# Shared experts' units spread past the mixer loop, the carried part of y scaled on ScalarE, x's normalised rows one chunk an iteration

## The chip, the cores and the metric

One core of one Trainium2 chip runs the whole program. The metric is device microseconds of one execution; the time before is the median of three runs. In the text PE is TensorE, PEld its weight loads, DVE VectorE, ACT ScalarE, POOL GpSimd, SP SyncE.

## The reference, cut to what matters

8 sequences of 1,024 tokens, model width 128. A Mamba-2 mixer (4 heads of 64, state 128), a residual with layer norm, a mixture of experts (14 routed with top 2, and 2 shared, hidden width 256), and a residual with layer norm again:

```python
zxbcdt = x @ in_proj_w                      # z 256, xBC 512, dt 4
xBC = silu(conv4(xBC) + conv_b)
# per token: state = state * exp(A dt) + (x dt) B ;  y = C . state
g = (y + D x) * silu(z);  g = g * rsqrt(mean(g**2) + eps) * norm_w
x = layernorm(x + g @ out_proj_w)
shared = sum over 2 experts of  silu(rmsnorm(x) * rw @ W1) @ W2
routed = gated sum over the top 2 of 14 experts of the same
x = layernorm(x + shared + routed)
```

## The kernel before

The 8,192 tokens are 64 chunks of 128 (`NC`), eight chunks a sequence (`CPB`), four chunks a tile (`NT` = 16 tiles). Every engine has its own program, written out by hand, and all run the same loop: iteration `i` from -5 to 83 (`LAST` = 84), in which each step works on a chunk or tile that lies a fixed number of iterations back. The order in which steps stand in the loop is the order of each engine's queue, and semaphores tie the engines together.

**The mixer, iterations up to 66.** In iteration i PE projects z of chunk i-1 (line 761), turns x and B of chunk i token-major (768), projects one of four 128-channel blocks of a tile (776), turns the gated g of chunk i-4 (782), does one unit of the shared experts, the out projection of chunk i-5 (809), and then the scan in its chunk form: gram (844), addition to the state (847), and y of chunk i-2 (857, 860), to which the carried part, the state times C, is written in the other half of the same PSUM bank (864; not in a sequence's first chunk). ACT empties z (946) and x and B (955, four instructions of 64 columns, each scaled by a per-partition dt; 958), applies the convolution's first tap and silu (971, 975, 963), sums g squared (980), copies gT (983), applies silu to the unit's hidden values (992). Every fourth iteration (i mod 4 = 3) it also writes the four normalised chunks of a tile into `rows` (1001, 1003) and normalises x itself in place, four instructions (909); one iteration later (i mod 4 = 0) it copies xnT (1009). DVE does three convolution taps (1117), the running decay (1125), the mix (1130), the state (1143), and for chunk i-3 y: the carried part times `into` (1151), plus the inside part (1154), times silu(z) (1160). `in_turn` takes one instruction of each of these chains in rotation.

**Units of the shared experts.** Unit u (`shared_units`) does on PE the first product of hidden block u (802, two matmul records) and, from u = 4 on, the second product of one chunk of the tile before (793, eight records). There are 68 units, one an iteration in iterations 16 to 83.

**PSUM banks.** `act_ring` and `dve_ring` give three banks each in the order in which uses are listed (`act_uses`, `dve_uses`). A use waits until the use three places before it has been released. So PE's gT (782) waits for ACT's zs of the same iteration (946), and PE's hidden product (802) for ACT's bt of the same iteration (958).

**The routed part.** Slots of 128 rows are read back from DRAM sorted by expert (`slots_in`), four tiles a group, 36 groups (`gr`). Groups 0 to 10 have their steps in iterations 69, 71, 73, 75 and 77 to 83, the rest stand behind the loop. A group costs PE four transposes (717), 8 hidden matmuls (728, 16 records) and 8 down matmuls (748, 16 records), ACT two silus (920), DVE two PSUM copies and four weight picks (1396, 1408, 1419), and POOL four indirect DMAs (602) that return the rows to DRAM. During the last iterations POOL also issues the indirect DMAs that dispatch rows (661). `xT`'s memory is used again by the routed part, once the hidden products that read it are done (`AREA_UNITS`).

Of the kernel before, what the change touches and what calls it, by code (L numbers as in the profile page):

```python
# [11 lines left out]
ALU = mybir.AluOpType  # L12
ACT = mybir.ActivationFunctionType
AX = mybir.AxisListType
P = 128
# [17 lines left out]
    "mix", "y_carried", "y_sum", "skip_diag", "gated", "residual", "ln_stats", "shift",  # L33
# [3 lines left out]
    "rate", "dt_exp", "chunk_decays", "step_decay", "rows_copied", "xbc_raw", "xbc_silu", "z_silu", "xdt", "g_squares", "bt",  # L37
# [34 lines left out]
def mamba_moe(nc, xT_d, x_d, w_in_d, conv_w_d, conv_b_d, norm_w_d, w_out_d, dt_bias_d, a_log_d,  # L72
# [75 lines left out]

    def shared_units(i):
        return [i - LAG] if 0 <= i - LAG < NC + 4 else []  # L150
# [66 lines left out]
    for gr in range(GROUPS_IN_LOOP, GROUPS):  # L217
        if gr + 2 < GROUPS:
            dve_uses.append(("slotsT", gr + 2))
        if gr + 1 < GROUPS:  # L220
            act_uses += [("routed", n2) for n2 in pairs_of(gr + 1)]
        dve_uses.append(("down", gr))

    with ExitStack() as ctx:
# [107 lines left out]
        carve, used = carver(xT[:])  # L332
        slots_out = [carve(W) for _ in range(3)]
# [339 lines left out]
        def tensor_program(e):  # L673
# [78 lines left out]

            dt_raws(*STEPS[0])
            for i in range(FIRST, LAST):
# [29 lines left out]
                for u in shared_units(i):  # L784
                    if u >= 4:
                        t, c4 = divmod(u - 4, 4)
                        on.wait_ge("hidden_silu", 4 * t + 4)
                        on.wait_ge("w2_loaded", 16)
                        on.wait_ge("shared_added", t)
                        on.wait_ge("dt_raw_added", 3)  # L790
                        for n in range(NSH):
                            e_no, k = divmod(n, HB)
                            mm = e.matmul(down_bank[:, c4 * P:(c4 + 1) * P], hid[(4 * t + n) % NHID][:, c4 * P:(c4 + 1) * P], w2_shared[:, e_no, k, :],  # L793
                                          start=(n == 0), stop=(n == NSH - 1))
                        mm.then_inc(S["down"])
                    if u < NC:
                        t, n = divmod(u, 4)
                        e_no, k = divmod(n, HB)
                        on.wait_ge("w1_scaled", NE - NR)
                        on.wait_ge("xnT_copied", t + 1)  # L800
                        bank = act_bank("hidden", u)
                        e.matmul(bank[:], w1_shared[:, e_no, k * P:(k + 1) * P], xnT[t], start=True, stop=True).then_inc(S["hidden"])  # L802
# [73 lines left out]
            for gr in range(GROUPS_IN_LOOP, GROUPS):  # L876
                routed_group(gr)
# [3 lines left out]
        def scalar_program(e):  # L881
# [53 lines left out]

            dt_exp(0)
            for i in range(FIRST, LAST):
# [46 lines left out]
                for u in shared_units(i):  # L984
                    if u < NC:
                        on.wait_ge("hidden", u + 1)

                        was = u - NHID
                        if was >= 0:
                            on.wait_ge("down", 4 * (was // 4) + 4)  # L990
                        on.wait_ge("dt_step", 3 * DT_CHAIN)
# [647 lines left out]
```

## Time and profile before

| | before |
|---|---|
| median of 3 runs (lowest, highest) | 784.41 us (782.98, 786.55) |
| the profiled execution's own time | 785.97 us |
| its span in the profile | 784.2 us |
| granted PE clock over the span | 0.924 |
| PE / PEld busy | 658.8 us (84%) / 557.2 us (71%) |
| DVE / ACT / POOL busy | 608.7 (78%) / 444.4 (57%) / 497.6 us (63%) |

Read it by stage: the mixer loop lies between about 60 and 470 us, the routed part behind it. A busy share over the whole span mixes the two. The profiled execution is 1.6 us above the median.

### The profile page before, as it was taken

To read this page: it belongs to the slowest core of one execution; us is meant where nothing else is said; L and a number is where in the kernel's file an instruction comes from. 1 tells how busy PE (TensorE), PEld (TensorE's weight loads), DVE (VectorE), ACT (ScalarE), POOL (GpSimd) and SP (SyncE) were. 2 spreads that over 40 slices of the span, in tenths; PEclk is the share of its full clock that TensorE was granted. 3 is DMA by queue.
4 is the path that set the end of the run, shared out by engine and by line. 5 is a ranking of instruction groups with operands and counts; after the bars stand their busy time and mean duration, and the time that the engine had idled before them with its cause. 6 is when DMAs were issued, how large, how long until landed. Compare 5 with 4: busy or idle time off the path is not lost.

```text
span 784.2 us, 14802 instructions
## 1 busy us (share of the span) xinstructions
PE 658.8 (84%) x4299; PEld 557.2 (71%) x4299; DVE 608.7 (78%) x1838; ACT 444.4 (57%) x1225; POOL 497.6 (63%) x545
## 2 busy tenths in 40 slices
PE   5987888999999999999999998886697877776840
PEld 4865676787787787787778887675587877665730
DVE  4899889999999999999999887337236342588875
ACT  4875777868767867877876754411113111335645
POOL 1144454887787787777887875566565656555652
PEclk9899999999999999999999999897799989898875
DMA  8541111121111221111221127123323222555436
GB/s 299 190 135 41 43 39 31 64 59 55 61 51 58 65 58 55 52 62 59 58 62 48 35 85 247 48 61 90 82 72 85 82 83 80 163 146 158 139 95 214
DMA packets 62639, 70.76 MB, mean 90 GB/s; under 512 B 10335, under 2 KB 45285, under 8 KB 62304
## 3 DMA queue, kind: packets, MB, share of 16 engines
q1 hardware_dynamic: 52656, 52.79, 23.2%
q0 software_dynamic: 8608, 16.87, 6.3%
q8 instruction: 36, 0.59, 0.3%
q14 instruction: 43, 0.35, 0.2%
q10 hardware_dynamic: 1296, 0.16, 0.1%
HBM read 48.55 MB, written 23.01 MB: 91 GB/s over the span
## 4 chain that ended last, share of the span: by engine, by line
PE 44%; issue 13%; ACT 11%; DVE 11%; another core or an unknown queue 4%; DMA 2%; SPq 2%; POOL 0%; DVEq 0%; ACTq 0%; POOLq 0%
PE bank L793 6%; PE bank L728 5%; PE bank L748 5%; PE bank L802 4%; PE bank L860 4%; ACT x L909 3%; PE bank L776 2%; PE bank L847 2%; ACT rows L1001 2%; PE bank L857 2%; PE bank L809 2%; PE bank L761 2%; PE bank L864 2%; DVE xbcT_area L1117 2%
## 5 line engine op out<-in xcount | busy, mean ns | idle before, releaser
L602 POOL DMA_INDIRECT returned<-xT,slots_in x141 | 142.7, 1012 | 102.5 <-DVE xT L1419 62.2
L661 POOL DMA_INDIRECT dispatched<-rows,row_u x128 | 147.2, 1150 | 31.6 <-issue 31.3
L1117 DVE SCALAR_TENSOR_TENSOR xbcT_area<-raw,conv_w,xbcT_area 128x512 f32<-128x512 f32 x162 | 125.5, 776 | 2.5 <-ACT xbcT_area L975 2.4
L728 PE MATMUL bank<-xT 128*128 128x128 f32 x564 | 85.0, 308 | 30.3 <-issue 12.8
L920 ACT ACTIVATE raw<-bank 128x512 f32<-128x512 f32 (+1 forms) x71 | 39.9, 588 | 117.2 <-remote 78.9
L728 PEld LDWEIGHTS bank<-xT 128*128 128x128 f32 x564 | 79.0, 221 | 34.6 <-issue 19.7
L1419 DVE COPY xT<-bank 128x512 f32<-128x512 f32 (+1 forms) x36 | 24.4, 678 | 101.1 <-remote 87.6
L748 PE MATMUL bank<-xbcT_area,raw 128*128 x564 | 83.3, 301 | 16.8 <-issue 16.0
L748 PEld LDWEIGHTS bank<-xbcT_area,raw 128*128 128x128 f32 x564 | 76.9, 214 | 20.6 <-issue 20.6
L1125 DVE TENSOR_TENSOR_SCAN decay_area<-decay_area,ident_heads 128x512 f32<-128x512 f32 x64 | 87.3, 1365 | 0.0
L946 ACT ACTIVATE zs<-bank 128x256 f32<-128x256 f32 x64 | 24.3, 379 | 110.0 <-PE bank L761 110.0
L793 PE MATMUL bank<-w_shared,hid 128*128 128x128 f32 x512 | 73.9, 284 | 13.5 <-issue 13.5
L793 PEld LDWEIGHTS bank<-w_shared,hid 128*128 128x128 f32 x512 | 66.6, 199 | 17.0 <-issue 16.8
L909 ACT ACTIVATE x<-x,shift,rstd 128x128 f32<-128x128 f32 x128 | 52.1, 480 | 39.4 <-issue 34.4
L649 POOL TENSOR_TENSOR state_kept<-state,whole 128x256 f32<-128x256 f32 x56 | 46.6, 833 | 41.2 <-DVE state L1143 25.5
L860 PE MATMUL bank<-xdt,mix 128*128 128x128 f32 x512 | 69.9, 281 | 0.0
L802 PE MATMUL bank<-xT,w_shared 128*128 128x512 f32 x128 | 68.3, 616 | 0.7 <-ACT bt L958 0.2
L776 PE MATMUL bank<-xT,w_in 128*128 128x512 f32 x128 | 66.9, 609 | 0.0
L593 POOL TENSOR_TENSOR xend<-xdt,outof 128x256 f32<-128x256 f32 x64 | 65.9, 1030 | 1.3 <-ACT xdt L955 1.2
L860 PEld LDWEIGHTS bank<-xdt,mix 128*128 128x128 f32 x512 | 64.6, 198 | 0.0
L955 ACT ACTIVATE xdt<-bank,dt 128x64 f32<-128x64 f32 x256 | 59.2, 313 | 1.6 <-PE bank L768 1.6
L992 ACT ACTIVATE hid<-bank 128x512 f32<-128x512 f32 x64 | 40.3, 629 | 33.0 <-remote 15.9
(232 smaller groups left out, 1531.0 us busy)
## 6 DMA issues: line engine op xcount, KB each, us to landing
decay_area<-decay_rows SPq DMA_DIRECT2D x64, 256.0 KB
slots_in<-dispatched SPq DMA_DIRECT2D x141, 64.5 KB
hid<-returned SPq DMA_DIRECT2D x18, 256.0 KB
xT<-xT_dram SPq DMA_DIRECT2D x8, 512.0 KB, 8.1
x<-x_dram SPq DMA_DIRECT2D x8, 512.0 KB, 7.9
out_dram<-x SPq DMA_DIRECT2D x16, 256.0 KB
xT<-returned SPq DMA_DIRECT2D x14, 256.0 KB
returned<-xT,slots_in POOLq DMA_INDIRECT x141
```

The source lines that it names most:

```text
L593: e.tensor_tensor(xend[h][:].rearrange("p (n s e) -> p n s e", s=2, e=HD), xdt[c % len(xdt)][:].rearrange("p n (s e) -> p n s e", e=HD)[:, ...
L602: e.indirect_dma_start(returned, bass.IndirectOffsetOnAxis(ap=slots_in[sb_][:, n, D:ROW].bitcast(U32), axis=0), slots_out[b][:, n * P:(n + ...
L661: e.indirect_dma_start(dispatched, bass.IndirectOffsetOnAxis(ap=row_u[t % 2][:, m:m + 1], axis=0), rows[t % 3][:, k, c4, :], None).then_in ...
L728: mm = e.matmul(bank[:, off:off + P], w1_now[b][:, k * P:(k + 1) * P], slotsT[gr % len(slotsT)][:, n % 4 * P:(n % 4 + 1) * P], start=True, ...
L748: mm = e.matmul(bank[:, j * P:(j + 1) * P], hidden_r[n2 % len(hidden_r)][:, off:off + P], w2_routed[:, bass.ds(experts[4 * (gr % 2) + j], ...
L776: e.matmul(bank[:], w_in[:, DI + k * P:DI + (k + 1) * P], xT[:, t * W:(t + 1) * W], start=True, stop=True).then_inc(S["xbc"])
L793: mm = e.matmul(down_bank[:, c4 * P:(c4 + 1) * P], hid[(4 * t + n) % NHID][:, c4 * P:(c4 + 1) * P], w2_shared[:, e_no, k, :], start=(n == ...
L802: e.matmul(bank[:], w1_shared[:, e_no, k * P:(k + 1) * P], xnT[t], start=True, stop=True).then_inc(S["hidden"])
L860: mm = e.matmul(bank[:, n * P:(n + 1) * P], mix[h][:, k, :], xdt[c % len(xdt)][:, n, zero_first * HD:zero_first * HD + P], start=False, st ...
L909: e.activation(x[:, 4 * t + c, :], x[:, 4 * t + c, :], ACT.Identity, scale=rstd[:, t, 0, c:c + 1], bias=shift[:, t, 0, c:c + 1]).then_inc( ...
L1117: e.scalar_tensor_tensor(o, r[:, n:n + W], conv_w[:, k, TAPS - 1 - n:TAPS - n], o, ALU.mult, ALU.add).then_inc(S["conv"])
L1125: e.tensor_tensor_scan(flat(running[c % 2]), flat(decay_all[b]), flat(ident_heads[:]), 0.0, ALU.mult, ALU.add).then_inc(S["running"])
```

## The change

Three edits, with nothing changed in what is computed.

1. `shared_units` follows a table: one unit an iteration, but none where i mod 4 = 3 up to iteration 64; two in iterations 68, 70, 72, 74 and 76; the last seven stand beside groups 11 to 17 behind the loop. At the end of iteration 64, 37 units are done where 49 were, and 61 at the end of iteration 83, where there were 68. The memory carved out of `xT` is ordered anew, with one wait for each piece.
2. The carried part times `into` moves from DVE (one instruction of 256 columns) to ACT (four instructions of 64 columns, one a head, per-partition scale), behind zs and ahead of xdt. DVE's addition now waits for ACT.
3. x is normalised one chunk an iteration, in iterations 12 to 75, instead of four chunks in each fourth iteration.

```diff
+    units = {i: 1 for i in range(LAG, LAST + NC) if i > NC or i % 4 != 3}
+    for i in range(NC + 3, min(ROUTED_AT[-1], NC + 13)):
+        if i not in ROUTED_AT:
+            units[i] = 2
+    unit_ends, units_so_far = {}, 0
+    for i in sorted(units):
+        units_so_far = min(units_so_far + units[i], NC + 4)
+        unit_ends[i] = units_so_far
+
     def shared_units(i):
-        return [i - LAG] if 0 <= i - LAG < NC + 4 else []
+        return range(unit_ends.get(i - 1, unit_ends.get(i - 2, 0)), unit_ends[i]) if i in unit_ends else []
+
+    def beside_group(gr):
+        return LAST + gr - GROUPS_IN_LOOP
...
@@ the memory carved out of xT
+        w1_now = [carve(HB * P) for _ in range(8)]
+        slotsT = [carve(W) for _ in range(3)]
+        SLOTST_UNITS = units_of(0)
+        OUT_UNITS = [units_of((b + 1) * W) for b in range(3)]
         slots_out = [carve(W) for _ in range(3)]
-        slotsT = [carve(W) for _ in range(3)]
-        w1_now = [carve(HB * P) for _ in range(8)]
         gexp = carve(NC * NR).rearrange("p (c r) -> p c r", c=NC)
-        AREA_UNITS = 4 * -(-used[0] // W)
+        GEXP_UNITS = units_of(0)
...
@@ TensorE (ScalarE and VectorE likewise)
             for gr in range(GROUPS_IN_LOOP, GROUPS):
+                shared_experts(beside_group(gr))
                 routed_group(gr)
...
@@ ScalarE
-            def normalise(t, signal):
-                for c in range(4):
+            def normalise(t, signal, chunks=range(4)):
+                for c in chunks:
...
+                c = i - 3
+                if at(i, 3, NC) and c % CPB:
+                    on.wait_ge("y_out", c + 1)
+                    on.wait_ge("chunk_decays", 3 * steps_range(c) + 3)
+                    on.wait_ge("y_sum", kept_upto(c) - 1)
+                    for k in range(NH):
+                        e.activation(y_carried[:, k * HD:(k + 1) * HD], dve_ring.bank("out", c)[:, DI + k * HD:DI + (k + 1) * HD], ACT.Copy,
+                                     scale=into[:, c, k:k + 1]).then_inc(S["y_carried"])
...
-                    normalise(t, "x1")
+                t, c = divmod(i - 12, 4)
+                if 0 <= t < NT:
+                    normalise(t, "x1", (c,))
...
@@ VectorE
                 if c % CPB:
-                    on.wait_ge("chunk_decays", 3 * steps_range(c) + 3)
-                    e.tensor_tensor(heads(y_carried[:]), heads(bank[:, DI:2 * DI]), per_head(into[:, c, :]), ALU.mult).then_inc(S["y_carried"])
-                    yield
-                    on.wait_ge("y_carried", kept_upto(c))
+                    on.wait_ge("y_carried", NH * kept_upto(c))
                     e.tensor_tensor(y_inside[:], bank[:, 0:DI], y_carried[:], ALU.add).then_inc(S["y_sum"])
```

ACT's queue in one iteration with i mod 4 = 3 and the start of the next, in the middle of the mixer, before:

```order
L946 ACTIVATE zs<-bank 128x256
L955 ACTIVATE xdt<-bank,dt 128x64 x4
L958 ACTIVATE bt<-bank 128x128
...
L983 ACTIVATE gT<-bank 128x256
L992 ACTIVATE hid<-bank 128x512
L1001 ACTIVATE rows<-x,shift,rstd 128x128 x4
L1003 ACTIVATE rows<-rows 128x4x128
L909 ACTIVATE x<-x,shift,rstd 128x128 x4
L946 ACTIVATE zs<-bank 128x256
```

The same stretch of the changed program:

```order
L982 ACTIVATE zs<-bank 128x256
L990 ACTIVATE y_carried<-bank,into 128x64 x4
L1000 ACTIVATE xdt<-bank,dt 128x64 x4
L1003 ACTIVATE bt<-bank 128x128
...
L1028 ACTIVATE gT<-bank 128x256
L1038 ACTIVATE rows<-x,shift,rstd 128x128 x4
L1040 ACTIVATE rows<-rows 128x4x128
L934 ACTIVATE x<-x,shift,rstd 128x128
L982 ACTIVATE zs<-bank 128x256
```

hid has left this iteration, three of the four x have gone to the other iterations, and four y_carried stand between zs and xdt in every iteration but one in eight.

PE's queue behind the loop, where group 11 follows group 10, before (the last down matmul of one group, then the next group):

```order
L748 MATMUL bank<-xbcT_area,raw 128x128
L717 MATMUL bank<-ident,slots_in 128x128 x4
L728 MATMUL bank<-xT 128x128 x8
L416 TENSOR_LOAD expert_late
```

and in the changed program a unit stands ahead of the group's transposes:

```order
L769 MATMUL bank<-xbcT_area,raw 128x128
L784 MATMUL bank<-w_shared,hid 128x128 x4
L793 MATMUL bank<-xT,w_shared 128x512
L738 MATMUL bank<-ident,slots_in 128x128 x4
L749 MATMUL bank<-xT 128x128 x8
L437 TENSOR_LOAD expert_late
```

Where a matmul has float32 operands, the trace shows two records for each of these rows' instructions.

## Rows read from the trace of the kernel before

**Rows 1.** Busy time by engine, four mixer iterations (start:end length, then engines)

```profile
293.00:321.00 28.00, 27.40 (x186) 22.18 (x183) 27.07 (x73) 21.07 (x63) 21.91 (x24) 1.00 0.18 55
```

**Rows 2.** Chain that ended last, 232 to 243 us (start, length, what)

```profile
232.65 0.43 PE bank L761 x2
...
236.89 0.49 ACT hid L992
...
239.85 1.17 ACT x L909 x3
241.02 0.36 ACT zs L946
...
242.81 0.86 PE bank L802 x2
```

**Rows 3.** Timeline of ACT, an iteration's start, and bt of an early one

```profile
311.39 0.38 ACT L946 ACTIVATE zs<-bank 128x256 f32<-128x256 f32 x1 [3.10 <-PE bank L761]
311.72 0.93 ACT L955 ACTIVATE xdt<-bank,dt 128x64 f32<-128x64 f32 x4
312.53 0.29 ACT L958 ACTIVATE bt<-bank 128x128 f32<-128x128 f32 x1
...
130.38 0.29 ACT L958 ACTIVATE bt<-bank 128x128 f32<-128x128 f32 x1
```

**Rows 4.** Timeline of PE: z and hidden product of these two iterations

```profile
310.76 0.59 PE L761 MATMUL bank<-w_in,xT 128*128 128x256 f32 x2
...
313.49 1.02 PE L802 MATMUL bank<-xT,w_shared 128*128 128x512 f32 x2
...
130.81 1.10 PE L802 MATMUL bank<-xT,w_shared 128*128 128x512 f32 x2 [0.20 <-ACT bt L958]
```

**Rows 5.** Group of DVE's carried part (count, busy us, mean ns, idle before)

```profile
L1151 DVE TENSOR_TENSOR y_carried<-bank,into 128x256 f32<-128x256 f32 x56 | 22.3, 399 | 3.2 <-PE bank L864 3.1
```

**Rows 6.** Timeline of DVE in that iteration, state and carried part

```profile
309.19 0.42 DVE L1143 TENSOR_TENSOR state<-bank,state_kept 128x256 f32<-128x256 f32 x1 [0.64 <-PE bank L847]
...
311.33 0.40 DVE L1151 TENSOR_TENSOR y_carried<-bank,into 128x256 f32<-128x256 f32 x1
```

**Rows 7.** Timeline of POOL, first and last of two bursts of eight DMAs

```profile
643.60 1.07 POOL L602 DMA_INDIRECT returned<-xT,slots_in  x1 [2.99 <-DVE xT L1419]
652.73 0.97 POOL L602 DMA_INDIRECT returned<-xT,slots_in  x1 [0.30 <-issue]
656.67 1.07 POOL L602 DMA_INDIRECT returned<-xT,slots_in  x1 [2.96 <-DVE xT L1419]
```

**Rows 8.** Timeline of PE over the first of these bursts

```profile
643.93 1.06 PE L717 MATMUL bank<-ident,slots_in 128*128 128x128 f32 x4
644.79 3.21 PE L728 MATMUL bank<-xT 128*128 128x128 f32 x16
647.84 1.95 PE L748 MATMUL bank<-xbcT_area,raw 128*128 x16
649.62 0.60 PE L717 MATMUL bank<-ident,slots_in 128*128 128x128 f32 x4
650.06 1.95 PE L728 MATMUL bank<-xT 128*128 128x128 f32 x16
652.98 0.27 PE L748 MATMUL bank<-xbcT_area,raw 128*128 x1 [0.44 <-issue]
655.13 1.48 PE L748 MATMUL bank<-xbcT_area,raw 128*128 x11 [0.44 <-issue]
```

**Rows 9.** Timeline of DVE: the copy that ends this wait

```profile
655.20 0.69 DVE L1419 COPY xT<-bank 128x512 f32<-128x512 f32 x1 [8.54 <-remote]
```

**Rows 10.** Chain that ended last, one unit in iteration 70

```profile
493.27 0.89 PE bank L793 x8
494.17 0.86 PE bank L802 x2
```

**Rows 11.** Timeline of PE: its wait behind the tables of iteration 76

```profile
547.73 3.75 PE L728 MATMUL bank<-xT 128*128 128x128 f32 x16 [4.80 <-DVE xT L1396]
```

More of the change, by code:

```diff
@@ L217, in mamba_moe @@
     for gr in range(GROUPS_IN_LOOP, GROUPS):
+        act_uses += [("hidden", u) for u in shared_units(beside_group(gr)) if u < NC]
         if gr + 2 < GROUPS:
@@ L751, in routed_group, with shared_experts @@
                 mm.then_inc(S["routed_down"])
+            def shared_experts(i):
+                for u in shared_units(i):
+                    if u >= 4:
+                        t, c4 = divmod(u - 4, 4)
+                        on.wait_ge("hidden_silu", 4 * t + 4)
+                        on.wait_ge("w2_loaded", 16)
+                        on.wait_ge("shared_added", t)
+                        on.wait_ge("dt_raw_added", 3)
+                        for n in range(NSH):
+                            e_no, k = divmod(n, HB)
+                            mm = e.matmul(down_bank[:, c4 * P:(c4 + 1) * P], hid[(4 * t + n) % NHID][:, c4 * P:(c4 + 1) * P], w2_shared[:, e_no, k, :],
+                                          start=(n == 0), stop=(n == NSH - 1))
+                        mm.then_inc(S["down"])
+                    if u < NC:
+                        t, n = divmod(u, 4)
+                        e_no, k = divmod(n, HB)
+                        on.wait_ge("w1_scaled", NE - NR)
+                        on.wait_ge("xnT_copied", t + 1)
+                        bank = act_bank("hidden", u)
+                        e.matmul(bank[:], w1_shared[:, e_no, k * P:(k + 1) * P], xnT[t], start=True, stop=True).then_inc(S["hidden"])
             dt_raws(*STEPS[0])
@@ L783, in tensor_program @@
                     tr.then_inc(S["gT"])
[L784 to L802, printed above, removed]
+                shared_experts(i)
                 c = i - 5
@@ L934, in by_token, with hidden_of_shared @@
                     normalise(s - 2, "x2")
+            def hidden_of_shared(i):
+                for u in shared_units(i):
+                    if u < NC:
+                        on.wait_ge("hidden", u + 1)
+                        was = u - NHID
+                        if was >= 0:
+                            on.wait_ge("down", 4 * (was // 4) + 4)
+                        on.wait_ge("dt_step", 3 * DT_CHAIN)
+                        e.activation(hid[u % NHID][:], act_ring.bank("hidden", u)[:], ACT.Silu).then_inc(S["hidden_silu"])
             dt_exp(0)
@@ L983, in scalar_program @@
                     e.activation(gT[c % 2][:].rearrange("p k i -> p (k i)"), act_ring.bank("gT", c)[:, 0:DI], ACT.Copy).then_inc(S["gT_copied"])
[L984 to L991, printed above, removed]
-                        e.activation(hid[u % NHID][:], act_ring.bank("hidden", u)[:], ACT.Silu).then_inc(S["hidden_silu"])
+                hidden_of_shared(i)
                 t = due(i, 11)
@@ L1417, in routed_group @@
                     on.wait_ge(f"returned{b}", 64 * (gr // len(slots_out)))
+                on.wait_ge("hidden", OUT_UNITS[b])
                 cols = slice(0, len(slot_tiles(gr)) * P)
@@ L1423, in gates_before @@
                 best = top_v[:, :, 0:1]
+                on.wait_ge("hidden", GEXP_UNITS)
                 e.tensor_tensor(rms_of[:], rstd[:, :, 0, :], rstd[:, :, 1, :], ALU.mult).then_inc(S["gate"])
@@ L1509, in by_token, with shared_add @@
                             ln_shift(u, 1, 3 * NT + 2 * n + 2)
+            def shared_add(i):
+                for u in shared_units(i):
+                    if u >= 4 and u % 4 == 3:
+                        t = (u - 4) // 4
+                        on.wait_ge("down", 4 * t + 4)
+                        on.wait_ge("x1", 4 * t + 4)
+                        e.tensor_tensor(x[:, 4 * t:4 * t + 4, :], down_bank[:].rearrange("p (c d) -> p c d", c=4), x[:, 4 * t:4 * t + 4, :], ALU.add).then_inc(S["shared_added"])
             later = steps_of(0)
@@ L1559, in vector_program @@
                     ln_shift(t, 2, 3 * t + 3)
-                for u in shared_units(i):
-                    if u >= 4 and u % 4 == 3:
-                        t = (u - 4) // 4
-                        on.wait_ge("down", 4 * t + 4)
-                        on.wait_ge("x1", 4 * t + 4)
-                        e.tensor_tensor(x[:, 4 * t:4 * t + 4, :], down_bank[:].rearrange("p (c d) -> p c d", c=4), x[:, 4 * t:4 * t + 4, :], ALU.add).then_inc(S["shared_added"])
+                shared_add(i)
                 if i == NC + 2:
@@ L1572, in vector_program @@
                 if n == 1:
-                    on.wait_ge("hidden", AREA_UNITS)
+                    on.wait_ge("hidden", SLOTST_UNITS)
                     for gr in range(2):
@@ L1583, in vector_program @@
                     gates_before()
+                shared_add(beside_group(gr))
                 routed_group(gr)
```

7 lines of the change are left out of this document (5 added, 2 removed).

## The prediction

> **What bounds the kernel now.** I read the busy time by stage first, then the chain that ended last, then the timelines around the waits in that chain. The reader should see that no engine has room to spare in the mixer on average, but that the chain changes engine in one iteration of four.
>
> In four mixer iterations PE is busy for 27.40 of 28.00 us and DVE for 27.07, while ACT works for 21.07 [rows 1]. So PE and DVE look like the bound. The chain says where the small rest is lost. In an iteration with i mod 4 = 3 ("the heavy iteration") it goes from PE's z at 232.65 to ACT and stays there, through hid and x at its end, until zs of the next iteration at 241.02; then PE's gT can start and at 242.81 the hidden product [rows 2]. From there it stays on PE for three iterations. One round of four iterations is thus an ACT stretch of 241.02 - 232.65 = 8.37 us and a PE stretch of the rest.
>
> Behind the loop POOL sets a rhythm: eight DMAs from 643.60 to 652.73 + 0.97 = 653.70, then a wait of 2.96 for DVE's copy, and the next burst at 656.67, a period of 13.07 us for two groups [rows 7]. PE issues 4 + 16 + 16 + 4 + 16 = 56 records in the burst, then goes on one by one, and resumes at 655.13, 1.4 us after POOL's last DMA; DVE's copy comes at 655.20, long after the down product of 647.84 was issued [rows 8, 9]. So in a burst PE can run ahead by some 56 records and then stands until POOL is through. The trace doesn't say why. The Trainium skill (TensorE: Matmul & The Clock Gate, Specifications) gives an engine queue depth of 64 for TensorE; by that rule the 56 records agree with a queue that fills up.
>
> **Edit 1, the units, in the mixer.** A round loses one unit: 8 records of the down product (0.89) and 2 of the hidden product (0.86), 1.75 us of PE [rows 10], and ACT's hid (0.49) in the heavy iteration [rows 2]. PE's part of it comes off at a place where the chain is on ACT, so only the 0.49 counts. What is late next is ACT's own queue.
>
> **Edit 3, x one chunk an iteration.** Three of four x leave the heavy iteration: 1.17 us off the ACT stretch [rows 2]. In the other three iterations ACT waits for PE's z (3.10 us in one of them [rows 3]), which hides the 0.39 that each gets; without that cover it would cost 1.17 a round and give the whole gain back.
>
> **Edit 2, the carried part on ACT.** DVE loses an instruction of 0.40, 56 times, 22.3 us [rows 5]. The new work on ACT is four instructions of 64 columns from PSUM with a per-partition scale, which is the form of xdt: four of them take 312.53 - 311.72 = 0.81 us of the queue [rows 3]. I take that. The end above it is four mean durations without overlap, 0.93 and more; the end below is nothing, if ACT waited anyway. They stand between zs and xdt, so everything behind zs comes 0.81 later: xdt, bt, silu, raw and the rest, and PE's hidden product waits for bt.
> The Trainium skill (ScalarE: Activation LUTs, What ACT_TABLE_LOAD costs) gives 186 ns, plus 93 for a pointer operand, plus 0.833 ns a column, less 93 of overlap: an estimate of 239 ns, 0.96 for four. The trace has 0.81; with 0.96 the mixer would come out 6 us dearer than below.
>
> How late is bt for PE? From zs's start to bt's end ACT needs 312.53 + 0.29 - 311.39 = 1.43 us [rows 3]; from bt's end to the hidden product, when it waits for it, 130.81 - 130.67 = 0.14 [rows 3, 4]. With the new 0.81 the hidden product can start 1.43 + 0.14 + 0.81 = 2.38 after zs.
> - Heavy iteration into the next: before, the hidden product came 242.81 - 241.02 = 1.79 behind zs [rows 2]; now 2.38, so 0.59 later.
> - The two other iterations with a unit: zs starts 0.63 behind z, the hidden product 2.73 behind z [rows 3, 4]. Now 0.63 + 2.38 = 3.01: a new wait of 0.28 in each.
>
> A round: -0.49 (hid) - 1.17 (x) + 0.81 (carried part in the heavy iteration) + 0.59 + 2 x 0.28 = +0.30. In every second round the heavy iteration's chunk is the first of a sequence and has no carried part: -0.51. The mean is -0.11, and 11 rounds (iterations 20 to 63) give -1.2 us. The 1.75 us that PE no longer works and the 0.40 of DVE turn into waits for ACT.
>
> Does DVE bound it? It gains 0.40 in three to four iterations of a round [rows 5], but its addition can't start before ACT's carried part is done, 0.63 + 0.33 + 0.81 = 1.77 behind PE's z, which here is at 312.53 [rows 3, 4]. DVE began this iteration at 309.19, ahead of z, and reached the carried part at 311.33 [rows 6], so it would wait 1.2 us there, with the mix queued behind it. Its gain pays for that; I count zero, also for the first iterations (3 to 19), where DVE is the fuller engine; bounds -5 to +4 for the whole mixer.
>
> **Edit 1, behind the mixer.** 12 units more stand after iteration 64: 12 x 1.75 = 21 us of PE at the full clock, if nothing hides them. Piece by piece:
> - Iteration 68, second unit: PE is in the chain there, as in iteration 70 [rows 10]. +1.75.
> - 70, 72, 74: each stands ahead of a group's down product, in a rhythm that POOL's bursts set. PE has about 13.07 us and needs about 8.4 for two units, a group and the small products; with a third unit 10.2. It then runs into the limit of 56 records before the down product is out, and gives 10 records after the burst. I take +1.2 for the three together (bounds 0 and 5.3).
> - 76: PE waits 4.80 us for the tables [rows 11], which hides 1.75. 0. Without that wait it would cost 1.75.
> - Groups 7 to 10 get a hidden product each (4 x 0.86 = 3.4), where PE already does a down product beside each group and a pair of groups takes about what POOL's bursts give. Half: +1.7.
> - Groups 11 to 17 get 3 whole units and 4 without a hidden product, 3 x 1.75 + 4 x 0.89 = 8.8. A pair has 72 records now, and some 82 find room in a period (56 in the burst, the rest in the 3 us between bursts at 0.11 each); a pair with units has 92 or 88. A third of the time: +2.9.
> Sum +7.6; bounds 1.75 and 21. The value is nearer the low end because POOL's 13.07 us stay as they are. The new wait values on the `xT` memory are met: 40 units are done by iteration 67, where 28 are asked for.
>
> **Sum.** -1.2 + 7.6 = +6.4 us. On the profiled execution's 785.97 us (span 784.2) that is 792.4; it lies 1.6 above the median, so the median should go from 784.4 to 790.8, say 791.
>
> **Rivals.**
> - *The mixer is freed after all.* If ACT keeps up (bt isn't late, or the heavy iteration's ACT stretch is hidden by PE's shorter queue), PE sets the round: 27.40 - 1.75 = 25.65 in place of 28.0, -2.35 a round over 12 rounds, -28 at most. It decides as soon as the ACT stretch of the heavy iteration falls under PE's. For it: ACT idles a quarter of the time [rows 1]. Against: the order in ACT's queue worked out above. With half of it and the tail's +7.6 the time is 784.4 - 14 + 7.6 = 778, in full 764.
> - *POOL's rhythm hides the units.* Only iteration 68 costs: -1.2 + 1.75 = +0.5, 785: no change. For it: the down product is issued long before the copy that waits for it [rows 8, 9].
> - *The units behind the mixer are all on the path*, as PE's record limit in a burst makes each cost more than its own time: +21, or 804.
> - *The edits don't do what they say* in the mixer, DVE's wait for ACT passes on to the mix and to PE: one wait of 1 us a round, +11, with the tail 802. The start of DVE's iteration ahead of z speaks for it, its idle time against.
>
> **How the numbers follow.** About 0.5% (3.9 us) is what a measurement of this kernel can tell from no change. Forecast (788.5 to 797): 0.42. Rhythm hides the units: 0.23. Mixer freed: 0.22. The two dear cases together: 0.13. Slower is the forecast and the dear cases less a tenth of the first's low edge, 0.52; same 0.26; faster 0.22. The range takes half of the freed mixer's cases and reaches to the dear ones: 774 to 803.
>
> **What the profile of the changed kernel would show.** Right: PE's round stays at 28 us with 25.6 busy; PE's hidden product waits for ACT's bt in most iterations; ACT's heavy iteration is followed by zs without idle time; DVE's addition waits for y_carried; the granted clock stays 1.00 in the mixer; iteration 64 ends about as early as before; POOL's bursts still come every 13 us and the last one ends 6 us later. Wrong: a round clearly under 28 us, or bursts whose period has grown by more than 1 us. The prediction fails most easily in the tail, where the third and the half are choices, and in the mixer if PE's longer waits let the clock fall.

## The result

| | before | after |
|---|---|---|
| median (lowest, highest), 4 runs each | 783.69 us (782.70, 786.55) | 811.28 us (808.27, 812.01) |
| the profiled execution / its span | 785.97 / 784.2 us | 812.01 / 810.2 us |
| zs of iteration 20 / of iteration 64 | 156.25 / 461.05 | 156.98 / 480.56 |
| a round of four iterations between them (11 rounds) | 27.71 us | 29.42 us |
| first / last DMA of the returned rows | 494.99 / 765.47 | 517.02 / 791.02 |

The changed kernel takes 1.0345 times as long (95%: 1.0313 to 1.0377), 27.6 us between the medians and 26 between the two profiled executions. By stage: +19.5 us up to iteration 64, +2.5 from there to the first returned row, +4.0 from there to the end. Nearly all of the surprise is in the mixer.

The view of busy time of the changed kernel over those 11 rounds answers to [rows 1]:

```profile
156.98:480.56 323.58, 297.11 (x1855) 243.38 (x1854) 271.60 (x757) 249.54 (x814) 233.97 (x258) 0.96 0.17 52
```

PE has 122 matmul records fewer than before (1855 against 1977) and is still busy for 297 us, at a granted clock of 0.96, and idle for 26.5. The view of waits (total us, times, longest) of the same stretch says for whom:

```profile
ACT zs L982 <- PE bank L803: 64.7, 38, 3.5
DVE y_inside L1192 <- ACT y_carried L990: 37.8, 22, 3.0
...
PE bank L868 <- DVE mix L1171: 22.8, 11, 2.9
```

DVE waits for ACT's carried part in two iterations of four, and once a round PE waits 2.1 us for DVE's mix, ahead of the gram. In the kernel before PE hardly waited for the mix (view of waits, iterations 20 to 64):

```profile
PE bank L844 <- DVE mix L1130: 0.5, 2, 0.3
```

The timelines of ACT and PE in a non-heavy iteration answer to [rows 3, 4]:

```profile
311.33 0.38 ACT L982 ACTIVATE zs<-bank 128x256 f32<-128x256 f32 x1 [1.65 <-PE bank L803]
311.61 0.92 ACT L990 ACTIVATE y_carried<-bank,into 128x64 f32<-128x64 f32 x4
312.39 0.95 ACT L1000 ACTIVATE xdt<-bank,dt 128x64 f32<-128x64 f32 x4
313.18 0.34 ACT L1003 ACTIVATE bt<-bank 128x128 f32<-128x128 f32 x1
```

```profile
310.70 0.59 PE L803 MATMUL bank<-w_in,xT 128*128 128x256 f32 x2
...
313.56 1.13 PE L793 MATMUL bank<-xT,w_shared 128*128 128x512 f32 x2
```

The four new instructions take 312.39 - 311.61 = 0.78 us (0.81 forecast), bt ends 2.19 behind zs (2.24 forecast), and the hidden product starts 2.86 behind z (3.01 forecast). ACT's queue is as I drew it. What I had not drawn comes in the next iterations, in DVE's timeline and then PE's:

```profile
320.26 0.42 DVE L1192 TENSOR_TENSOR y_inside<-bank,y_carried 128x256 f32<-128x256 f32 x1 [1.05 <-ACT y_carried L990]
...
321.38 0.68 DVE L1171 TENSOR_TENSOR mix<-decay_area,bank 128x512 f32<-128x512 f32 x1
...
325.76 1.63 DVE L1166 TENSOR_TENSOR_SCAN decay_area<-decay_area,ident_heads 128x512 f32<-128x512 f32 x1
...
328.29 0.67 DVE L1171 TENSOR_TENSOR mix<-decay_area,bank 128x512 f32<-128x512 f32 x1
```

```profile
329.11 0.46 PE L868 MATMUL bank<-xbcT_area 128*128 128x128 f32 x2 [1.98 <-DVE mix L1171]
```

DVE waits at its addition, and the mix of the same iteration stands behind it. From there DVE works almost without a gap (the router's choice is in this iteration), and its next mix ends 8.7 us after the start of the addition, when PE has been standing for 1.98. This is the heavy iteration, the one that lost its unit, so PE gets to the gram 1.75 us sooner than before. This trace alone doesn't say how much of PE's wait comes from DVE's wait and how much from the missing unit; e2 and e4 below do. And PE's wait has a price of its own. Two of the eleven waits in PE's timeline:

```profile
182.47 0.35 PE L868 MATMUL bank<-xbcT_area 128*128 128x128 f32 x1 [1.73 <-DVE mix L1171]
240.14 0.35 PE L868 MATMUL bank<-xbcT_area 128*128 128x128 f32 x1 [2.14 <-DVE mix L1171]
```

and the 4.5 us behind each of them and behind a third, in the view of busy time (the granted clock is the third number from the right):

```profile
182.47:186.97 4.50, 4.50 (x29) 3.77 (x30) 3.07 (x5) 4.47 (x16) 4.02 (x6) 1.00 0.21 75
240.14:244.64 4.50, 4.50 (x20) 4.25 (x21) 3.07 (x5) 2.99 (x9) 4.02 (x6) 0.62 0.25 70
449.05:453.55 4.50, 4.50 (x20) 4.20 (x21) 2.07 (x3) 1.16 (x3) 3.86 (x7) 0.63 0.19 61
```

The third wait was of 2.90 us. After the first the clock stays at its upper level (2.4 GHz) and 29 records fit; after the others it is 0.62 on average, most of the stretch at 1.2 GHz, and 20 fit. Seven of the eleven waits are followed by such a stretch (those of 2.14, 2.33, 2.71 and 2.90 us and three of 1.98), four are not (1.55, 1.55, 1.73 and one of 1.98): 7 x 4.5 x 0.38 = 12 us. The Trainium skill (TensorE: Matmul & The Clock Gate, HAM oscillation) describes a matmul kernel whose groups are parted by waits for DMA and start at the throttled clock each time. The trace agrees that waits which come back regularly are paid for in clock again and again; the waits in the page's example are longer than these, and that such a stretch can follow waits of 1.98 to 2.90 us is shown by this trace alone.

So the 18.8 us between iterations 20 and 64 are: PE's idle time from 5.3 to 26.5 (+21.1), the clock +12, units gone 11 x 1.75 = -19.3, and +5 that remain. The hidden product, which waits for bt, accounts for 3 of them: it is busy for 36.84 us in 33 units where it was for 45.04 in 44, that is 1.12 for 1.02 each. The other 2 I can't place.

Behind the loop POOL's timeline answers to [rows 7]: bursts of eight as before. The two shown lie 13.36 us apart; from any burst of eight to the next burst it is 13.0 to 13.5 us in both kernels, once 14.5 in the changed one.

```profile
694.86 1.07 POOL L623 DMA_INDIRECT returned<-xT,slots_in  x1 [2.89 <-DVE xT L1458]
...
703.89 0.97 POOL L623 DMA_INDIRECT returned<-xT,slots_in  x1 [0.30 <-issue]
708.22 0.97 POOL L623 DMA_INDIRECT returned<-xT,slots_in  x1 [3.36 <-issue]
```

### The profile page after: what moved, and what is told of

The parts are those of the page before. It is cut to its first block, busy times and chain, and to the rows that moved or that the text cites. A ratio compares the mean times of both kernels' runs of the same rounds, so it can differ in the third digit from the quotient of the medians.

```text
span 810.2 us, 15029 instructions
## 1 busy us (share of the span) xinstructions
PE 668.1 (82%) x4299; PEld 562.6 (69%) x4299; DVE 584.5 (72%) x1782; ACT 489.1 (60%) x1449; POOL 486.3 (60%) x545
## 4 chain that ended last, share of the span: by engine, by line
PE 43%; DVE 21%; ACT 15%; issue 14%; DMA 2%; another core or an unknown queue 2%; SPq 1%; DVEq 0%; POOL 0%; ACTq 0%; POOLq 0%
DVE xbcT_area L1158 5%; PE bank L769 5%; PE bank L749 5%; PE bank L884 5%; PE bank L784 5%; PE bank L793 5%; ACT y_carried L990 3%; PE bank L881 2%; DVE decay_area L1166 2%; PE bank L871 2%; DVE mix L1171 2%; PE bank L803 2%; PE bank L888 2%; ACT xdt L1000 2%
## 5 line engine op out<-in xcount | busy, mean ns | idle before, releaser
L682 POOL DMA_INDIRECT dispatched<-rows,row_u x128 | 143.5, 1121 | 31.7 <-issue 31.7
L1158 DVE SCALAR_TENSOR_TENSOR xbcT_area<-raw,conv_w,xbcT_area 128x512 f32<-128x512 f32 x162 | 123.3, 762 | 3.3 <-ACT xbcT_area L1020 3.3
L749 PE MATMUL bank<-xT 128*128 128x128 f32 x564 | 83.3, 306 | 26.8 <-issue 12.0
L769 PE MATMUL bank<-xbcT_area,raw 128*128 x564 | 81.5, 300 | 8.4 <-issue 7.4
L934 ACT ACTIVATE x<-x,shift,rstd 128x128 f32<-128x128 f32 x128 | 61.0, 515 | 39.4 <-DVE shift L1525 27.5
L793 PE MATMUL bank<-xT,w_shared 128*128 128x512 f32 x128 | 72.4, 647 | 7.9 <-ACT bt L1003 4.4
L884 PE MATMUL bank<-xdt,mix 128*128 128x128 f32 x512 | 73.4, 290 | 0.0
L884 PEld LDWEIGHTS bank<-xdt,mix 128*128 128x128 f32 x512 | 68.3, 207 | 0.0
L614 POOL TENSOR_TENSOR xend<-xdt,outof 128x256 f32<-128x256 f32 x64 | 61.3, 957 | 0.2 <-ACT xdt L1000 0.2
```

The costliest lines, as they stand in the source:

```text
L614: e.tensor_tensor(xend[h][:].rearrange("p (n s e) -> p n s e", s=2, e=HD), xdt[c % len(xdt)][:].rearrange("p n (s e) -> p n s e", e=HD)[:, ...
L682: e.indirect_dma_start(dispatched, bass.IndirectOffsetOnAxis(ap=row_u[t % 2][:, m:m + 1], axis=0), rows[t % 3][:, k, c4, :], None).then_in ...
L749: mm = e.matmul(bank[:, off:off + P], w1_now[b][:, k * P:(k + 1) * P], slotsT[gr % len(slotsT)][:, n % 4 * P:(n % 4 + 1) * P], start=True, ...
L769: mm = e.matmul(bank[:, j * P:(j + 1) * P], hidden_r[n2 % len(hidden_r)][:, off:off + P], w2_routed[:, bass.ds(experts[4 * (gr % 2) + j], ...
L884: mm = e.matmul(bank[:, n * P:(n + 1) * P], mix[h][:, k, :], xdt[c % len(xdt)][:, n, zero_first * HD:zero_first * HD + P], start=False, st ...
L1158: e.scalar_tensor_tensor(o, r[:, n:n + W], conv_w[:, k, TAPS - 1 - n:TAPS - n], o, ALU.mult, ALU.add).then_inc(S["conv"])
```

## The experiments

Four groups of four, each group on one chip with the kernel before beside it (medians of before: 738.95, 781.93, 782.33 and 787.22 us). "Round" is the time of four iterations, the mean of the 11 rounds between zs of iterations 20 and 64; it hardly depends on the chip (27.71 and 27.69 for the kernel before, 27.06, 27.06 and 27.02 for the third edit alone). The times expected for e1 to e4 are for a kernel before of 784 us; their chip runs it in 738.95, so the ratio is what can be compared.

| run | what | ratio to before [95%] | round, us | zs of iteration 64 |
|---|---|---|---|---|
| e5 | before again | | 27.69 | 460.74 |
| e2 | edit 1 | 1.0006 [0.9990, 1.0023] | 27.35 | 456.07 |
| e1 | edit 2 | 1.0332 [1.0292, 1.0373] | 29.35 | 483.58 |
| e3, e11, e16 | edit 3 | 0.9852 [0.9810, 0.9895], 0.9895 [0.9872, 0.9917], 0.9865 [0.9841, 0.9889] | 27.06, 27.06, 27.02 | 450.28, 451.56, 451.03 |
| e4 | edits 1, 3 | 0.9926 [0.9901, 0.9951] | 27.07 | 452.27 |
| e10 | edits 2, 3 | 1.0140 [1.0115, 1.0165] | 28.51 | 472.02 |
| after | all | 1.0345 [1.0313, 1.0377] | 29.42 | 480.56 |
| e6 | all, mix first | 1.0110 [1.0084, 1.0135] | 27.84 | 463.09 |
| e7 | all, carried part ahead of zs | 1.0098 [1.0069, 1.0126] | 27.84 | 463.42 |
| e9 | all, both moves | 0.9998 [0.9981, 1.0015] | 27.31 | 452.61 |
| e8 | edits 2, 3, mix first | 1.0107 [1.0075, 1.0139] | 28.22 | 465.29 |
| e12 | edits 2, 3, both moves | 0.9957 [0.9940, 0.9975] | 27.54 | 457.44 |
| e13 | edits 1, 3, unit from i mod 4 = 1 | 0.9890 [0.9862, 0.9919] | 26.71 | 446.03 |
| e14 | all, both moves, unit from 1 | 0.9831 [0.9805, 0.9858] | 26.22 | 442.08 |
| e15 | all, both moves, unit from 2 | 0.9882 [0.9856, 0.9909] | 26.49 | 446.31 |

### Each edit alone

**e1**, the carried part alone, the `+` lines of ScalarE and the `-` lines of VectorE in the diff above:

```diff
-                    e.tensor_tensor(heads(y_carried[:]), heads(bank[:, DI:2 * DI]), per_head(into[:, c, :]), ALU.mult).then_inc(S["y_carried"])
-                    yield
+                        e.activation(y_carried[:, k * HD:(k + 1) * HD], dve_ring.bank("out", c)[:, DI + k * HD:DI + (k + 1) * HD], ACT.Copy,
```

> The kernel before with the second edit alone (the carried part on ScalarE). Theory A, the carried part on ACT is the cause of the loss in the mixer (DVE's addition waits for ACT, the mix is queued behind it, PE's gram waits for the mix) and of the late start of the slots' loads (the early table's steps are queued behind the same wait): nearly all of the changed kernel's +11 us up to iteration 64 and +8 us behind it are here too, and ACT's heavy iteration keeps its three other x, so 800 to 812. Rival B, the loss comes from the units that were moved out of the heavy iterations (PE reaches gram too early and then waits, the work comes back later): this kernel is then within 4 us of the kernel before, 780 to 788.

As large a loss is here without the two other edits: iteration 64 comes 22.8 us later than in e5. (The expectation gives the changed kernel's loss as 11 and 8 us; its trace has 19.5 and 6.5.) DVE's wait is as in the changed kernel (view of waits, iterations 20 to 64), and PE waits for bt, which it did nowhere before:

```profile
DVE y_inside L1160 <- ACT y_carried L954: 40.8, 22, 2.8
...
PEld bank L802 <- ACT bt L967: 10.3, 35, 0.6
...
PE bank L802 <- ACT bt L967: 4.2, 10, 0.5
...
PE bank L844 <- DVE mix L1139: 2.3, 6, 1.1
```

But the mechanism of theory A is not what costs in this run: PE hardly waits for the mix, since the heavy iteration still has its unit. The round is 1.66 us longer than in e5, and the prediction's own terms for edit 2 (0.81 in every second heavy iteration, 0.59 and 2 x 0.28) make 1.56 a round. ACT's added work and the late bt are thus nearly the whole of it.

**e2**, the units alone:

```diff
+    units = {i: 1 for i in range(LAG, LAST + NC) if i > NC or i % 4 != 3}
```

> The kernel before with the first edit alone (the units moved, with the order of the memory areas and the waits that belong to it). Theory A: the mixer gets no slower (iteration 64 at most 2 us from the kernel before, or earlier), the slots' loads start on time, and the units cost only behind the mixer, 2 us in iteration 68 and 4 in the routed groups: 786 to 791. Rival B: iteration 64 comes 8 to 12 us late here too, 798 to 810.

No change: a round is shorter by 0.35, and the units cost again behind the mixer what that gave. Rival B is out as the cause of the loss. But the missing unit by itself makes PE wait for the mix, with the carried part still on DVE (view of waits, iterations 20 to 64):

```profile
PE bank L868 <- DVE mix L1159: 15.3, 11, 2.0
```

**e3**, the third edit alone:

```diff
-                    normalise(t, "x1")
+                t, c = divmod(i - 12, 4)
+                if 0 <= t < NT:
+                    normalise(t, "x1", (c,))
```

> The kernel before with the third edit alone (the residual's normalised rows one chunk an iteration). Theory A: three x (1.17 us) leave the ACT stretch of the heavy iteration and the others are hidden by ACT's wait for z: up to -1.17 x 15 rounds, so 767 to 783. Rival: PE's own work of 27.4 in 28.0 us a round leaves only 0.6 a round to gain, 776 to 783; or ACT's wait for z was not free and nothing changes, 783 to 786.

Faster, and bound by PE: 27.06 us a round, with PE busy for 295.93 of 297.62 us in this view of busy time.

```profile
152.66:450.28 297.62, 295.93 (x1973) 245.07 (x1972) 291.41 (x803) 225.09 (x669) 244.15 (x256) 1.00 0.18 56
```

**e4**, the changed kernel with the carried part back on VectorE.

```diff
-                    on.wait_ge("y_carried", NH * kept_upto(c))
+                    e.tensor_tensor(heads(y_carried[:]), heads(bank[:, DI:2 * DI]), per_head(into[:, c, :]), ALU.mult).then_inc(S["y_carried"])
```

> The changed kernel with the carried part back on VectorE, so the first and the third edit. Theory A: ACT's stretch of the heavy iteration is 1.66 us shorter and PE's round has 1.75 less to do; the mixer comes out 5 to 25 us earlier, the units cost 4 to 6 behind it: 765 to 785, faster than the kernel before. Rival B, the moved units are what costs: 800 or more.

Faster than before, and slower than e3. The surprise is that the round is the same as in e3 though PE works 16 us less. Busy time and the wait that took the work's place:

```profile
154.49:452.27 297.78, 280.13 (x1855) 233.36 (x1854) 286.30 (x798) 220.19 (x658) 239.98 (x254) 0.99 0.18 56
```

```profile
PE bank L868 <- DVE mix L1162: 17.3, 11, 2.6
```

The unit's time in the heavy iteration became a wait for the mix, one for one. The changed kernel differs from e4 in edit 2 alone: the carried part costs the mixer 480.56 - 452.27 = 28 us when added to edits 1 and 3, which without it gain 8.5. Over the 11 rounds it is 25.8 us. PE's idle time grows by 8.8 of them, its wait for the mix (17.3 to 22.8) by only 5.5; about 9 are the clock (0.99 here, 0.96 there), and some 8 are longer records of PE, with the hidden product waiting for bt. So most of PE's wait for the mix comes from the missing unit, and DVE's wait lengthens it to where the clock falls often.

### The place of the wait

**e5** is the kernel before again.

> The kernel before once more, one look, so that its stages stand beside those of the other kernels on the same chip. Both theories: rounds of four iterations 27.4 to 27.8 us long.

27.69, as the first profile.

**e6** puts one turn into DVE's chain, so that the next tap and the mix go ahead of the addition; ACT is untouched.

```diff
                 if c % CPB:
+                    yield
                     on.wait_ge("y_carried", NH * kept_upto(c))
```

> The changed kernel with one turn more in VectorE's chain ahead of the addition that reads y_carried, so that the next tap and the mix come before it, as they did in the kernel before; ACT's work is the same. Theory C, the loss is the place of the waiting instruction in DVE's order (mix and everything of PE that needs it stand behind a wait for ACT): the wait goes, a round is then bound by PE's and DVE's own work of 25.3 to 25.7 us and takes 25.7 to 26.5, and the whole is faster than the kernel before by 1 to 4%. Rival D, the loss is ACT's extra 0.8 us an iteration, wherever DVE waits: rounds of 28.5 to 29.5 and 2.5% to 3.5% slower than before, as the changed kernel.

One line gives back 17.5 us of the mixer. The view of waits, iterations 20 to 64:

```profile
DVE state L1184 <- PE bank L871: 18.1, 14, 2.2
...
PE bank L868 <- DVE mix L1171: 10.6, 10, 1.9
...
PEld bank L793 <- ACT bt L1003: 7.4, 26, 1.5
```

DVE's wait for ACT is no longer among the large ones, PE's wait for the mix is halved, and the granted clock is 1.00 over the stretch: no wait was followed by a slow stretch. The clock is 12 of the 17.4 us that the 11 rounds got shorter. Theory C had the cause right and the size too good, 27.84 and not 26.5 at most, and a whole that is 1.1% slower than before and not 1% to 4% faster: PE still waits 10.6 us for the mix, DVE 18.1 for PE's addition to the state, and the hidden product for bt.

**e7** leaves DVE's order and moves ACT's four instructions ahead of zs (y_out is written just before z, so they can run while z is).

```diff
+                (the carried part's block, c = i - 3)
                 c = i - 1
                 if at(i, 1, NC):
                     on.wait_ge("z", c + 1)
-                (the carried part's block, behind zs)
```

> The changed kernel with ACT's carried part ahead of zs instead of behind it; DVE's order is the changed kernel's. Theory C: DVE's addition can start some 0.35 to 0.9 us earlier behind PE's y_out, so the wait gets shorter and a round 0.4 to 1.2 us shorter than the changed kernel's 29.4, still not under before: 1% to 2.5% slower than before. Rival D: ACT's work is the same, zs and so gT come 0.35 later, no gain: 3% or more slower.

The same 27.84 by the other road. DVE's wait is halved and PE's for bt is nearly gone (1.1 us in all); PE's wait for the mix stays, and with it part of the slow clock (0.98 over the stretch):

```profile
DVE y_inside L1192 <- ACT y_carried L985: 19.3, 21, 2.2
PE bank L868 <- DVE mix L1171: 18.9, 11, 2.6
```

The gain of 1.58 us a round is above my upper end of 1.2; the ratio is at the end of what I expected. ACT's work is the same in after, e6 and e7, so rival D, the work alone wherever it stands, falls. The work isn't free either: with both moves (e9) a round is still 0.24 us longer than e4's, and without the moved units (e12) 0.48 longer than e3's.

**e8** is edits 2 and 3 with the mix first, without the moved units.

> The kernel before with the second and the third edit and the extra turn on VectorE, without the moved units. Theory C: the mixer is bound by PE's own 27.06 us a round, as with the third edit alone, and DVE's freed time brings nothing: 1.3% to 1.8% faster than before. Rival D: as slow as with the second edit alone, 2% to 3.5% slower.

A miss for theory C: 28.22, not 27.06; with 1.1% slower it isn't rival D's 2% to 3.5% either. Here PE is in the chain throughout, and seven of eight hidden products take 1.11 us in it in place of 0.86 (the eighth is in a heavy iteration without a carried part), behind a heavy iteration with up to 0.41 of waiting ahead of them. The chain, and the view of waits between 156 and 453 us:

```profile
300.93 0.41 issue
301.35 1.12 PE bank L802 x2
...
308.90 1.11 PE bank L802 x2
```

```profile
PEld bank L802 <- ACT bt L967: 7.6, 33, 0.6
```

That is the 0.28 an iteration of my prediction, measured at 0.25, and the 0.59 behind the heavy iteration, measured at 0.41 + 0.26 where it is shown. Over the 11 rounds PE is busy for 10.0 us more than in e3 and idle for 2.9 more, 0.91 + 0.26 a round, which is the 1.16 that the round is over e3's.

**e9**, both moves in the changed kernel.

> The changed kernel with both moves: ACT's carried part ahead of zs, and the mix ahead of the addition on VectorE. Theory C: each alone left a round of 27.84 us; the first takes away bt's lateness (2.9 + 7.4 us of PE's waits), the second DVE's waits for ACT (19.3 us), so together the round is 26.4 to 27.3 and the whole 0% to 1% faster than before, as the moved units still cost 7 behind the mixer. Rival E: what is left is DVE's own chain of state, tap, scan, tap and mix in the heavy iteration, which neither move shortens: again 27.5 to 27.9 a round and 0.7% to 1.2% slower than before.

27.31 and no difference from before: theory C, at its edge. What is left is the heavy iteration on ACT again, here in a stretch of the chain that ended last:

```profile
314.13 1.53 ACT rows L1038 x4
...
316.60 0.91 ACT y_carried L985 x4
317.51 0.28 ACT zs L991
...
317.84 0.44 PE bank L824 x2
```

**e10**, edits 2 and 3, nothing moved.

> The kernel before with the second and the third edit, the addition at the changed kernel's place in VectorE's order, the units not moved. It differs from the changed kernel by the moved units alone, and from the run with the mix first by that order alone. Theory C: with its unit in place PE comes to the heavy iteration's gram 1.75 us later, so most of the wait of 2 us for the mix is covered by work: a round takes 28.2 to 28.8 and the whole 1% to 2% slower than before. Rival F, the wait of DVE for ACT costs the same with or without the units: a round of 29.4 and 2.5% slower or more.

28.51, as theory C said: with its unit in place PE isn't at the gram early, and edit 1 adds 0.9 us a round to edits 2 and 3 where it adds nothing to edit 3 and takes 0.35 from before. The place of the addition, too, counts for little with the unit in place: 28.51 here and 28.22 in e8, 0.29 a round, where with the units moved it was 1.58 (after and e6). A clock below 1.00 over the 11 rounds is seen only where the heavy iteration has lost its unit (0.99 in e2, e4 and e9, 0.98 in e7, though 1.00 in e6); with the late mix beside it, in the changed kernel, it falls most (0.96).

**e11** is the third edit again; **e16** below is so too.

> The third edit alone once more, beside the others on this chip. A round is bound by PE's own 27.06 us; the mixer ends 10.5 us earlier than before and the routed groups are as before: 1.2% to 1.6% faster. Rival: on a chip where POOL's bursts set the groups' time the gain is lost behind the mixer, 0 to 0.8% faster.

The mixer ends 9.2 us earlier than in e5, and the whole is 8.1 us faster, 1.05%: between my two ranges. Some of the gain is lost behind the mixer here; on the first chip it was 1.5%.

**e12**, edits 2 and 3 with both moves.

> The second and the third edit with both moves, the units not moved. Theory C: bt isn't late any more (in the run with the mix first alone PE waited 0.25 to 0.41 us for it in every iteration, 28.22 a round), so a round is PE's own 27.06 us and the time is that of the third edit alone, 1.2% to 1.6% faster than before. Rival E: zs is now what comes late for PE's transposes of g, and a round takes 27.6 to 28.2.

27.54, just under rival E's range: bt is on time, but now PE's transposes of g wait for zs behind the heavy iteration, and a round is 0.5 us over e3's. Without moved units the carried part on ACT doesn't pay at any place that I tried, since PE is the bound (busy for 298.4 of 303.0 us in e12) and DVE's freed time is worth nothing.

### Which iteration gives up its unit

**e13** is e4 with another remainder.

```diff
-    units = {i: 1 for i in range(LAG, LAST + NC) if i > NC or i % 4 != 3}
+    units = {i: 1 for i in range(LAG, LAST + NC) if i > NC or i % 4 != 1}
```

> The first and the third edit, with the unit taken from the iterations with i mod 4 = 1 instead of 3; the carried part on VectorE. Theory G, VectorE's whole work bounds the round: 26.8 to 27.2 us again, PE's wait for the mix only stands elsewhere, and the whole 0.4% to 0.9% faster than before. Theory H, the place counts: PE reaches the mix of the iteration with i mod 4 = 3 later, the wait goes, and a round takes 25.8 to 26.5, the whole 1.5% to 2.5% faster.

26.71, between the two theories' ranges: the place is worth 0.36 a round. DVE is busy for 287.45 of 293.81 us and PE idle for 14.3, so DVE's own work seems to hold the rest; no run shows that by itself.

**e14** and **e15** are e9 with the remainder 1 and 2.

> The changed kernel with both moves (carried part ahead of zs, mix ahead of the addition) and the unit taken from the iterations with i mod 4 = 1. Theory G: VectorE's work is 25.6 a round, so the round comes under 27.06, 26.2 to 26.9. Theory H: 25.7 to 26.3. Rival: ACT's stretch of the heavy iteration, with its hid back, bounds it, 27.3 to 27.9.

> As the run before, with the unit taken from the iterations with i mod 4 = 2. Theory G: 26.2 to 26.9 a round as well. Theory H: the iteration ahead of the heavy one loses PE's cover while VectorE does the router's choice, 26.9 to 27.6. Rival, ACT's heavy stretch: 27.3 to 27.9.

e15 takes 26.49 a round, so the iteration ahead of the heavy one can give up its unit too (theory H said 26.9 or more); e14, with 26.22, has the shortest round of all and is the fastest against the kernel before. Theory G's range holds both rounds, but 26.22 lies in theory H's as well, so e14 doesn't part the two. Its busy time, and its wait for the mix:

```profile
153.61:442.08 288.47, 280.24 (x1856) 229.84 (x1855) 278.92 (x759) 249.05 (x815) 241.30 (x256) 1.00 0.20 58
```

```profile
PE bank L868 <- DVE mix L1171: 5.2, 10, 0.9
```

> The third edit alone, beside the three others: a round of 27.06 us and 1% to 1.5% faster than before.

On this chip e14's runs (773.13 to 775.17 us) lie below all of e16's (776.40 to 779.46): the three edits, with both instructions moved and the unit taken from another iteration, beat the kernel before by 1.7% and the third edit alone by 0.4%. The mixer ends 8.95 us earlier than in e16, and the moved units take 3.6 of that back behind it.

## Why the prediction was wrong

- **The sum:** +6.4 forecast, +26 measured between the profiled executions (27.6 between the medians), outside my range of 774 to 803. That the sign came out right is luck in the main: the term that gave it, behind the mixer, is a quarter of the loss, and the mixer, at -1.2, had the wrong sign.
- **The step that failed** is "Does DVE bound it? ... Its gain pays for that; I count zero", with bounds of -5 to +4 and so a mixer of -1.2. The mixer measured +19.5. I had the wait (1.2 us forecast, 1.05 in the iteration shown, 37.8 in all) and had even written that the mix stands behind it. I then paid for it with the 0.40 that DVE had gained, as if a wait could be paid for by work saved elsewhere on the engine. e6 measures the step: with ACT's work unchanged and the mix ahead of the wait, the 11 rounds are 17.4 us shorter, 12 of them by the clock. It costs this only together with edit 1; with the units in place (e10 against e8) it is 3 us, within my bounds.
- **Edit by edit**, us a round: edit 3 -1.17 forecast, -0.65 measured (e3 against e5); edit 2 on top of it +1.56 forecast, +1.45 measured (e10 against e3); edit 1 on top of both -0.49 forecast, +0.91 measured (the changed kernel against e10). So 0.5 of the 1.8 us a round that I missed is edit 3, and the rest is edit 1 meeting the late mix.
- **ACT's work by itself** (+0.81, bt late by 0.28): right, measured at 0.78 and, in e8, 0.25 an iteration.
- **Edit 1 in the mixer**, "only the 0.49 counts": near by itself (e2: -0.35 a round); that PE's 1.75 would turn into waits for ACT was wrong. They turned into waits for DVE's mix (e2, e4), and with the mix late these grew so long that the clock fell seven times, 12 us that I had only named as a way to fail.
- **Edit 3:** I counted 1.17 us off ACT's heavy stretch. Alone it gave 0.65 a round, since PE's own 27.06 are reached first (e3).
- **Behind the mixer:** +7.6 forecast, +6.5 between the two profiled executions (up to the first returned row 1.75 forecast and 2.5 measured, after it 5.8 and 4.0; against e5 in place of the first profile it is 2.7 and 7.0, so executions of one kernel differ by 3 us here). The last burst is 6 us later when counted from iteration 64, and the period stays near 13 us, both as forecast. No run tests the pieces of this sum, the halves and thirds above all, so that it came out near may be luck.
- **The rivals:** "the edits don't do what they say" named the mechanism, one wait a round passed on through the mix, and priced it at 1 us a round; PE's wait for the mix is 2.1 a round and the whole mixer lost 1.7. It shared the smallest chance, 0.13, with another. "The mixer is freed" is what the same edits do in e14, with two instructions moved and another iteration lightened: 27.71 -> 26.22.

## What to carry to other kernels

When work moves from one engine to another, price the new wait by what is queued behind the waiting instruction, not by its own length, and don't set saved work on that engine against it: look for the first instruction behind it that a third engine needs, and put that ahead. Work taken out of an iteration helps only if the engine's next operand is early there (in the heavy iteration it wasn't, e4; taken from another it gained 0.36 us a round, e13); choose the iteration by that. Before counting a wait of PE at its own length, look whether waits that long are followed by a slower clock in the same trace.

## What the hardware showed beside this

The first four runs were on a chip on which every kernel was some 45 us faster, before included (738.95), nearly all of it behind the mixer (e3 has a span of 725.2 us and e11, the same kernel, one of 772.0, with iteration 64 at 450.28 and 451.56). POOL's group of returned rows, e3's line and then e11's (count, busy us, mean ns, idle before):

```profile
L602 POOL DMA_INDIRECT returned<-xT,slots_in x141 | 141.8, 1006 | 54.7 <-issue 40.4 <-DVE xT L1422 14.3
```

```profile
L602 POOL DMA_INDIRECT returned<-xT,slots_in x141 | 142.9, 1014 | 96.8 <-DVE xT L1422 53.5 <-issue 43.3
```

The DMAs are as long, but on the second chip POOL waits 39 us more for DVE. PE's timeline beside an unbroken row of POOL's DMAs in e3:

```profile
603.08 0.60 PE L717 MATMUL bank<-ident,slots_in 128*128 128x128 f32 x4
603.52 1.95 PE L728 MATMUL bank<-xT 128*128 128x128 f32 x16
605.30 1.95 PE L748 MATMUL bank<-xbcT_area,raw 128*128 x16
607.09 0.60 PE L717 MATMUL bank<-ident,slots_in 128*128 128x128 f32 x4
607.53 1.95 PE L728 MATMUL bank<-xT 128*128 128x128 f32 x16
609.31 1.95 PE L748 MATMUL bank<-xbcT_area,raw 128*128 x16
```

and in e11:

```profile
636.59 0.27 PE L748 MATMUL bank<-xbcT_area,raw 128*128 x1 [0.95 <-issue]
637.32 0.27 PE L748 MATMUL bank<-xbcT_area,raw 128*128 x1 [0.45 <-issue]
638.74 0.37 PE L748 MATMUL bank<-xbcT_area,raw 128*128 x1 [1.16 <-issue]
```

On the first chip PE runs these 72 records on end while POOL issues, with no sign of the limit of some 56 records that [rows 8] showed and on which part of my tail estimate rested; every trace from the others has it in most of the bursts of eight, though not in all. What makes the chips differ no run here settles. The moved units cost on both: from iteration 64 to the end of the span, e4 took 280.4 us and e3 274.9 on the first, e14 330.3 and e16 326.7 on a later one.
